# Toeplitz convolution of a gated attention kernel: the lower left 4x4 blocks by 12 block products with a shared term

## What is computed

```python
kv = jnp.einsum('bhil,bhjl->bijhl', k_, v_)
y = irfft(rfft(kv, n=2*L) * rfft(ssm_kernel, n=2*L), n=2*L)[..., :L]
out = y + kv * D[None, None, None, :, None]
out = jnp.einsum('bijhl,bhil->bjhl', out, q_)
x = x + jnp.tanh(g_xattn[0]) * out
```

## Time and profile before

| | |
|---|---|
| median of 3 runs | 1708.61 us (1708.61 to 1708.88) |
| the profiled execution | 1702.75 us, its span 1700.9 us |
| PE busy | 1553.1 us (91%) |
| DVE busy | 1232.6 us (72%) |
| POOL busy | 948.3 us (56%) |
| ACT busy | 538.7 us (32%) |
| mean granted clock of PE | 0.95 |

### The profile page before, as it was taken

One profiled execution on the slowest core, in us unless ns is written; L12 is line 12 of the kernel. 1 busy time (PEld: TensorE's weight loads), 2 busy tenths in 40 slices (PEclk: granted clock), 3 DMA queues, 4 the chain that ended last, 5 costly groups with the idle time before them and its releaser, 6 DMA issues. The chain is left out here.

```text
span 1700.9 us, 32688 instructions
## 1 busy us (share of the span) xinstructions
PE 1553.1 (91%) x11300; PEld 1494.9 (88%) x11301; DVE 1232.6 (72%) x1829; ACT 538.7 (32%) x848; POOL 948.3 (56%) x633
## 2 busy tenths in 40 slices
PE   5999999999999999999999999747999999996553
PEld 5999999999999999999999999647999999895332
DVE  4878888888888888888888888594444444444798
ACT  3333433333343334333333433203333333331000
POOL 6667757766775776577567757052222222232465
PEclk9999999999999999999999999857999999998586
DMA  5554554555455555545554554234788888885999
GB/s 182 166 178 158 172 170 163 177 177 175 154 170 167 173 165 189 165 152 174 173 176 157 181 167 146 79 133 137 251 291 311 288 305 292 299 276 196 411 396 360
DMA packets 101006, 350.84 MB, mean 206 GB/s; under 512 B 11953, under 2 KB 12465, under 8 KB 100977
## 3 DMA queue, kind: packets, MB, share of 16 engines
q1 hardware_dynamic: 71024, 241.39, 42.5%
q0 software_dynamic: 29952, 109.07, 18.0%
HBM read 236.58 MB, written 113.84 MB: 206 GB/s over the span
## 5 line engine op out<-in xcount | busy, mean ns | idle before, releaser
L584 PE MATMUL Y<-kvhi,t_hi 128*128 128x288 f32 x2304 | 689.4, 299 | 3.2 <-DMA t_lo<-klo 1.9
L584 PE MATMUL Y<-kvlo,t_hi 128*128 128x288 f32 x2304 | 679.9, 295 | 0.0
L584 PE MATMUL Y<-kvhi,t_lo 128*128 128x288 f32 x2304 | 679.8, 295 | 0.0
L584 PEld LDWEIGHTS Y<-kvhi,t_hi 128*128 128x128 f32 x2304 | 433.0, 188 | 4.9 <-DMA t_lo<-klo 2.3
L584 PEld LDWEIGHTS Y<-kvlo,t_hi 128*128 128x128 f32 x2304 | 433.7, 188 | 0.0
L584 PEld LDWEIGHTS Y<-kvhi,t_lo 128*128 128x128 f32 x2304 | 433.5, 188 | 0.0
L440 DVE TENSOR_REDUCE oT<-z 128x128 f32<-128x1280 f32 x256 | 379.5, 1482 | 6.7
L269 POOL TENSOR_TENSOR kvlo<-kv,kvhi 128x1152 fp32r<-128x1152 f32 x128 | 341.3, 2691 | 4.1 <-ACT kvhi L306 4.1
L423 DVE TENSOR_TENSOR z<-Y,qT 128x512 f32<-128x512 f32 x256 | 175.9, 687 | 174.1 <-PE Y L584 174.1
L258 POOL TENSOR_TENSOR kv<-cT 128x1024 f32<-128x1024 f32 x128 | 291.7, 2279 | 8.7 <-DMA cT<-in_c 8.7
L306 ACT CAST kvhi<-kv 128x1152 fp32r<-128x1152 f32 x128 | 148.5, 1161 | 303.3 <-POOL kv L261 303.3
(11 more groups left out here) (151 smaller groups left out, 2149.8 us busy)
## 6 DMA issues: line engine op xcount, KB each, us to landing
made_rows<-made POOLq DMA_DIRECT2D x72, 512.0 KB
t_hi<-khi SPq DMA_DIRECT2D x64, 512.0 KB, 3.9
t_lo<-klo SPq DMA_DIRECT2D x64, 512.0 KB, 5.1
cT<-in_c SPq DMA_DIRECT2D x32, 768.0 KB, 6.4
x_nat<-in_x SPq DMA_DIRECT2D x32, 512.0 KB, 4.1
x<-x_new SPq DMA_DIRECT2D x32, 512.0 KB, 4.9
normed<-n SPq DMA_DIRECT2D x32, 512.0 KB, 3.0
w_raw<-in_w SPq DMA_DIRECT2D x32, 384.0 KB, 4.1
```

The source lines that it names most:

```text
L584: mm = nc.tensor.matmul(Y[s2][:, a, 0:YC], t[h][:, w], m[h][:, s, :], start=(s == 0 and t is t_hi and m is kvhi), stop=(s == c and t is t_lo))
```

## The change

The lower left 4x4 blocks of the Toeplitz matrix (outputs 4 to 7, inputs 0 to 3) are seen as a 2x2 matrix of groups G of 2x2 blocks, G4 and G2 in the upper row, G6 and G4 in the lower (the number is the distance in blocks). Then

```diff
-ORDER = (1, 2, 0, 3)
+ORDER = (1, 2, 3, 0)
...
-        kv = [sb(f"kv{h}", [P, NC, YC]) for h in range(HT)]
+        kv = sb("kv", [P, NC, YC])
...
+                    eng.dma_start(u_hi[h][:].bitcast(F32), kernel_window(kshi_d, n, KS, SW)).then_inc(t_in[h], 16)
+                    eng.dma_start(u_lo[h][:].bitcast(F32), kernel_window(kslo_d, n, KS, SW)).then_inc(t_in[h], 16)
...
+                def difference(n):
+                    eng.wait_ge(square_done, 2 * n + 1)
+                    if not (isinstance(n, int) and n < 1):
+                        eng.wait_ge(diffhi_done, n)
+                    nc.gpsimd.tensor_tensor(diff[:], kv[:, 0:2, :], kv[:, 2:4, :], ALU.subtract).then_inc(diff_done, 1)
...
+                def low_difference(n, h):
+                    eng.wait_ge(diffhi_done, n + 1)
+                    nc.gpsimd.tensor_tensor(diff_lo[h][:], diff[:], diff_hi[h][:].bitcast(F32),
+                                            ALU.subtract).then_inc(difflo_done[h], 1)
...
-                    products(2 * i + h, h, 0, p, have)
-                    products(2 * i + h, h, 1, p, have)
+                    products(i, h, 0, p, have)
+                    products(i, h, 1, p, have)
+                    difference(2 * i + h)
+                    if isinstance(i, int) and i == 0 and h == 1:
+                        eng.wait_ge(k_out, 64)
                     low_kv(2 * i + h, h)
+                    low_difference(2 * i + h, h)
...
+                def squares(n, p, h):
+                    eng.wait_ge(kv_done, 2 * n + 1)
                     for half in range(2):
                         c0 = half * (NC // 2)
+                        nc.scalar.activation(kv[:, c0:c0 + NC // 2, 0:IB], cT[p][:, h, c0:c0 + NC // 2, 0:IB],
+                                             ACT.Square).then_inc(square_done, 1)
...
+                def head(n, p, h):
+                    squares(n, p, h)
+                    high_kv(n, h, 0)
+                    high_kv(n, h, 1)
+                    high_difference(n, h)
+
+                def take_common(n, h):
+                    eng.wait_ge(shared_ready, n + 1)
+                    if not (isinstance(n, int) and n < HT):
+                        eng.wait_ge(joined, 2 * n - 2)
+                    nc.scalar.copy(common[h][:], shared_y).then_inc(common_done, 1)
...
                 def body(i, p, first=False, last=False):
+                    take_common(2 * i, 0)
                     high_w(i)
-                    high_kv(2 * i + 1, 1)
+                    head(2 * i + 1, p, 1)
+                    if not first:
+                        root2(i - 1)
+                        normalize2(i - 1, 1 - p)
                     if not (isinstance(i, int) and i < 2):
                         take_small(i - 2)
-                    if not first:
-                        root2(i - 1)
+                    take_common(2 * i + 1, 1)
                     if not last:
-                        high_kv(2 * i + 2, 0)
-                    if not first:
-                        normalize2(i - 1, 1 - p)
-                    if not last:
+                        head(2 * i + 2, 1 - p, 0)
                         root(i + 1)
-                        normalize(i + 1, 1 - p)
                     if not first:
                         high_n2(i - 1)
                     if not last:
+                        normalize(i + 1, 1 - p)
                         take_q(i + 1, 1 - p)
...
+                    if n in (1, 2):
+                        eng.wait_ge(common_done, 2 * i + h + 1)
+                        nc.vector.tensor_tensor(y, y, common[h][:], (ALU.add, ALU.subtract)[n - 1]).then_inc(joined, 1)
+                        eng.wait_ge(joined, 4 * i + 2 * h + n)
...
                     multiply(i, p, 0, 1)
                     total(i, p, 0, 1)
                     if not first:
-                        residual(i - 1, 1 - p)
-                    multiply(i, p, 0, 2)
-                    if not first:
                         stats2(i - 1, 1 - p)
                         eng.wait_ge(n2st_done, 3 * i - 2)
+                    multiply(i, p, 0, 2)
+                    if not first:
+                        aggregate2()
                     total(i, p, 0, 2)
                     if not first:
-                        aggregate2()
+                        invert2(i - 1)
                     multiply(i, p, 0, 3)
-                    if not first:
-                        invert2(i - 1)
+                    if not (isinstance(i, int) and i < 2):
+                        take_lr(i - 2)
+                    total(i, p, 0, 3)
...
+                    total(i, p, 1, 0)
+                    if not first:
+                        low_n2(i - 1)
+                    multiply(i, p, 1, 1)
...
+                    shared(i, 0)
+                    conv(i, 0, 0)
+                    if not first:
+                        transpose_o(i - 1, 1 - p)
+                    conv(i, 0, 1)
+                    conv(i, 0, 2)
+                    if not (isinstance(i, int) and i < 2):
+                        project(i - 2)
+                    conv(i, 0, 3)
+                    shared(i, 1)
+                    conv(i, 1, 0)
+                    if not first:
+                        transpose_n2(i - 1, 1 - p)
+                    conv(i, 1, 1)
+                    conv(i, 1, 2)
                     if not last:
                         transpose_x(i + 1)
+                    conv(i, 1, 3)
```

More of the change, by code:

```diff
@@ L94, in attend @@
         qT = [sb(f"qT{p}", [P, HT, NC, WR]) for p in range(2)]
-        kv = [sb(f"kv{h}", [P, NC, YC]) for h in range(HT)]
+        kv = sb("kv", [P, NC, YC])
         kvhi = [sb(f"kvhi{h}", [P, NC, YC], F32R) for h in range(HT)]
         kvlo = [sb(f"kvlo{h}", [P, NC, YC], F32R) for h in range(HT)]
-        t_hi = [sb(f"t_hi{h}", [P, L], F32R) for h in range(HT)]
-        t_lo = [sb(f"t_lo{h}", [P, L], F32R) for h in range(HT)]
+        diff = sb("diff", [P, 2, YC])
+        diff_hi = [sb(f"diff_hi{h}", [P, 2, YC], F32R) for h in range(HT)]
+        diff_lo = [sb(f"diff_lo{h}", [P, 2, YC], F32R) for h in range(HT)]
+        t_hi = [sb(f"t_hi{h}", [P, TW], F32R) for h in range(HT)]
+        t_lo = [sb(f"t_lo{h}", [P, TW], F32R) for h in range(HT)]
+        u_hi = [sb(f"u_hi{h}", [P, SW], F32R) for h in range(HT)]
+        common = [sb(f"common{h}", [P, 2, YC]) for h in range(HT)]
+        u_lo = [sb(f"u_lo{h}", [P, SW], F32R) for h in range(HT)]
         oT = [sb(f"oT{p}", [P, NC, P]) for p in range(2)]
@@ L143, in attend @@
         kvlo_done = [sem(f"kvlo_done{h}") for h in range(HT)]
+        square_done = sem("square_done")
+        diff_done, diffhi_done = sem("diff_done"), sem("diffhi_done")
+        difflo_done = [sem(f"difflo_done{h}") for h in range(HT)]
+        shared_ready, common_done = sem("shared_ready"), sem("common_done")
+        joined = sem("joined")
         y_ready = sem("y_ready")
@@ L165, in attend, with kernel_window @@
         q_done = sem("q_done")
[L167 to L169 removed]
+        def kernel_window(d, n, row, width):
+            return bass.AP(tensor=d.tensor, offset=n * row, ap=[[1, P], [1, width]])
         stored = [lambda i: 8 * i, lambda i: 8 * i - 8]
@@ L367, in _ @@
                 eng.wait_ge(k_sum, 1)
-                nc.scalar.copy(krow_hi[:], krow[:]).then_inc(khi_done, 1)
+                nc.scalar.copy(krow_hi, krow).then_inc(khi_done, 1)
+                eng.wait_ge(ks_sum, 1)
+                nc.scalar.copy(ksum_hi, ksum).then_inc(kshi_done, 1)
                 eng.wait_ge(const_in, 48)
@@ L531, in body @@
                         eng.wait_ge(st_done, 3 * i + 4)
-                    total(i, p, 0, 3)
+                    multiply(i, p, 1, 0)
                     if not last:
                         aggregate(i + 1)
-                    if not (isinstance(i, int) and i < 2):
-                        take_lr(i - 2)
-                    multiply(i, p, 1, 0)
+                    total(i, p, 1, 0)
+                    if not first:
+                        low_n2(i - 1)
+                    multiply(i, p, 1, 1)
                     if not last:
                         invert(i + 1)
-                    total(i, p, 1, 0)
-                    multiply(i, p, 1, 1)
                     total(i, p, 1, 1)
                     multiply(i, p, 1, 2)
-                    if not first:
-                        low_n2(i - 1)
                     total(i, p, 1, 2)
@@ L567, in _, with block, shared, plain @@
             def _(eng):
+                def block(out, w_hi, w_lo, d, m_hi, m_lo, c, start=False, stop=False):
+                    w = slice(d * P, (d + 1) * P)
+                    nc.tensor.matmul(out, w_hi[:, w], m_hi[:, c, :], start=start, stop=False)
+                    nc.tensor.matmul(out, w_hi[:, w], m_lo[:, c, :], start=False, stop=False)
+                    return nc.tensor.matmul(out, w_lo[:, w], m_hi[:, c, :], start=False, stop=stop)
+                def shared(i, h):
```

(35 more changed lines are left out.)

106 lines of the change are left out of this document (63 added, 43 removed).

## The result

| | before | changed |
|---|---|---|
| median | 1708.61 us | 1718.3 us (1717.02 to 1718.95) |
| ratio | | 1.0059, interval 1.0042 to 1.0077 |
| span of the profiled execution | 1700.9 us | 1717.0 us |
| PE / DVE / POOL / ACT busy | 1553 / 1233 / 948 / 539 us | 1498 / 1332 / 1068 / 656 us |
| mean granted clock of PE | 0.950 | 0.927 |

The changed kernel is slower by 0.6%; 1686 was forecast. The profiled execution of before was 6 us faster than its median, and its stages after the first took 598.5 us, where the traces of all the other kernels here, with the same code there, have 600.8 to 603.9. So of the 16.1 us between the two spans only 9.7 are in the difference of the medians.

The account below looks back on a forecast made before the run. The relay over ACT and POOL, with xn, was taken as the new bound: 32.3 us a tile against 33.27. Thirty tiles at 0.94 gain 28.2; with the ends the net is -22.5, so 1686 us, range 1660 to 1740.

Parts of the forecast that it names:

- The full 100 us of PE's queue: Matmuls on PE: queue falls 3.2 us to 29.95 a tile, 100 us if PE still set the pace.
- PE's own loop through the relay: PE's work together with the relay, from tile to tile: 32.1 us, next late after the loop of 32.3.
- the relay: From shared(i,0)'s end over ACT's take_common, w_hi and POOL's w_lo, products, difference, low_kv, low_difference to shared(i,1): 16.0 us.
- the relay with xn in it: Relay, then high_n2, DVE's low_n2 to invert, ACT's xn, transpose_x, next shared: 32.3 us a tile, the bound; chance 0.44.
- the join: DVE's add of 576 elements with one operand and result in PSUM, four a tile: 0.75 us each.
- rival 6: Table loads on ACT if Square lies outside Sqrt's table: +2.0 us a tile, +39 us, 1748; chance 0.06.
- The 0.24 for slower: Chance that the changed kernel is measured slower, from the join, clock and table load cases.
- the three rivals: The slower cases: join's PSUM read and write taking turns (0.10), PE's clock (0.07), ACT's table loads (0.06).
- rival 5: PE's clock falls to 1.2 GHz once a tile after 2.1 us idle: 34.0 a tile, +29 us, 1738; chance 0.07.
- the loops over xn: DVE's loop, queue 30.6 plus 0.8 idle and handoffs: 31.4 to 31.9; relay with xn: 32.3 a tile.
- rival 2: DVE or PE through the relay binds at 31.6 a tile, handoffs being shorter: 45 us less, 1664; chance 0.17.
- the ends: Stage's start and end: +4.6 start, +0.5 first tile, +0.6 tile 1, -1.2 last tile, +1.2 DVE's arrears.

Follow-up runs that it names:

- c1_invert: The changed kernel with one call moved: DVE's invert(i+1) ahead of low_n2; 1689.36 us, 0.9893 of the kernel before.
- b1_fill_order: a1_fill with DVE's invert(i+1) moved ahead of low_n2 and ACT's take_small ahead of root2; 1689.71 us, 0.9892 of the kernel before.
- a1_fill: The changed kernel with 12 extra matmuls a tile, result overwritten, in PE's idle time ahead of shared(i,1); 1699.26 us, 0.9956 of the kernel before.
- a2_relay: The changed kernel with ACT's high_w after head(2i+1) and POOL's low_w after head(i,1); 1690.83 us, 0.9906 of the kernel before.
- c4_halffill: a1_fill with 6 extra matmuls instead of 12, ahead of shared(i,1); 1699.4 us.
- a3_relay_nojoin: a2_relay with DVE's four joins a tile replaced by an operation on one element; 1682.09 us, 0.986 of the kernel before.

## Why the prediction was wrong

**Right.** The full 100 us of PE's queue did not come, because loops over other engines took over, and PE's own loop through the relay, forecast at 32.1, measures 32.31 (c1_invert) and 32.33 (b1_fill_order). That this equals the 32.3 forecast for another loop, the relay with xn in it, is luck: that loop takes 32.7 (below). Most terms held: the join 0.76 to 0.77 for 0.75, POOL's part of the relay 14.3 (498.85 to 513.19) for 14.2, its wait for w_hi 5.6 to 8.4 instead of 10.23, the first shared matmul at 25.48 for 25.8, 24 matmuls less a tile. PE idles 1.7 to 2.1 before shared(i,1), forecast 2.1. There are no loads of a table within the tiles, which ends rival 6. The Trainium skill (ScalarE: Activation LUTs, Table sets) has cheap functions in every set; the trace is in line with it, and shows of Square that it alternates with Sqrt here without a load. The 0.24 for slower holds the 0.01 of the change not doing what it says; the three rivals add up to 0.23.

**Wrong, first: rival 5, the clock, had a chance of 0.07.** I took the 2.21 us row, at full clock, as the nearest, read the 0.80 behind it as the end of a series, and so the sum priced the relay's idle time at nothing. That was a misreading: the row shows only the first matmul after the idle time, and the clock falls later. Windows of the kernel before (window, length, busy of PE, clock, DMA share, GB/s) around the row at 1627.61:

```profile
1627.00:1628.00 1.00, 0.40 (x2) 1.00 1.04 426
1628.00:1629.00 1.00, 1.00 (x6) 0.93 1.05 373
1629.00:1630.00 1.00, 0.48 (x2) 0.50 0.96 385
...
1631.00:1632.00 1.00, 0.31 (x1) 0.50 1.00 401
```

Some 1.3 us after PE had gone on the clock went to 0.50, and the 0.80 at 1631.69 was taken at that clock. In the changed kernel the falls come 1.0 to 1.4 us after PE has gone on, in 14 of 29 tiles. The size was off as well, in the other direction: a fall costs 1.24 us, not 1.9, since the low stretch is 3 us instead of 3.9 and a little of it runs under slack. 14 x 1.24 = 17 us in steady tiles; a1_fill shows 19 in all. The Trainium skill (TensorE: Matmul & The Clock Gate, HAM oscillation) had warned of idle time repeated in a loop, with a kernel whose waits took 3 to 5 us and whose every pass started cold. The trace agrees in part: falls came with 1.77 to 2.09 us, in 14 of 29 passes, and each pass started at full clock.

**Wrong, second: the loops over xn, a term of the sum.** DVE's was put at 31.4 to 31.9 and is 32.66. From one multiply of (0,0) to the next it runs 18.02 on DVE (500.29 to 518.31), 2.83, 1.14 and 2.06 to invert at 524.34, then 1.81 to transpose_x at 526.15 and 6.88 over the last convolution, shared and the next first convolution: 32.74. The prediction had summed DVE's queue and one wait and added half a microsecond for handoffs; laid out in order, two waits behind bn_stats (0.22 and 0.19), 0.9 instead of 0.8 at take_lr, and 8.7 us over ACT and PE were more than that. a2_relay is the proof: without the relay the tile stays at 32.65.

The relay with xn in it, which the sum took at 32.33, was short as well. In the same tile it takes 16.16 from the end of shared(i,0) at 497.13 to shared(i,1) (forecast 16.03), 12.86 to transpose_x (12.70) and 3.72 to the next end of shared (3.60): 32.74. The two loops meet in low_n2, and they are tied: DVE starts it 0.03 us after the end of ACT's n_hi in every tile, 0.03 to 0.05 later than its own queue would let it (1.43 to 1.45 after the start of the reduce, elsewhere 1.40). Timeline of ACT; low_n2 is the row at 521.14 above:

```profile
519.82 0.20 ACT L380 ACTIVATE low<-mv 128x1 f32<-128x1 f32 x1
...
520.11 0.99 ACT L428 CAST n_hi<-XP 128x1024 fp32r<-128x1024 f32 x1
```

At full clock ACT's part of this waits now for DVE, now for its own casts of the relay, with some 0.15 us at most between them. So shortening the relay alone gained nothing in a steady tile at full clock (a2_relay); shortening DVE's loop alone would gain some 0.1 us, an estimate from these rows that no run tests; c1_invert shortens both. The term costs 0.33 x 29 = 10 us. "DVE binds" stood as rival 2, but with the sign of a gain, at 31.6.

**Wrong, third: the ends.** Net +5.7 was said; the third take_q comes 8.4 us later than before (4.8 expected at that point) and the stage's last stretch is 4.0 us longer (0 expected). Low clock again: in tiles 0 and 1 stretches of 5.3 and 5.5 us at 0.50 follow PE's waits of 4.02 and 3.57 us. The runs fit this: with both stretches the third take_q is at 94.25 (c4_halffill), with one of some 3 us at 90.60 (a1_fill), with none at 85.76 (a2_relay). At the end one more fall comes in the last tile, PE waits longer for DVE, and it is slower in its transposes than before (2.97 and 1.58 us):

```profile
1098.91 1.97 PE L709 MATMUL OP<-const_ident,oT 128*128 128x128 f32 x8 [5.35 <-DVE oT L515]
```

The wait is 2.4 us longer than before; the prediction had put DVE's arrears at 1.2. No run takes the 4.0 us apart.

Together 10 + 17 + 3.6 + 4.0 = 35 us above a forecast of -22.5: +12 at the end of this stage, where the trace has +13.1. The other 3 us of the two spans are in the later stages, whose code is the same in both.

**The order of the calls decided the sign.** The same instructions with four calls moved (high_w, low_w, take_small, invert) take 1647.87, 3.5% less than the kernel before.

## What to carry to other kernels

Where one engine's queue is shortened, lay out every loop over the others in the order of their queues, with each handoff, before the gain is counted; the sum of a queue plus a lump for handoffs was short by 0.8 us in 32 here, and moving one call (invert, take_small, high_w with its low_w) was worth 15 to 29 us, but two of them together only some 10 where the relay stood close behind (b1_fill_order). Idle time of TensorE is not free where it stands off the critical loop: recurring in one piece of some 2 us it cost the clock here, and filling it, even by half, ended that. Read the clock of the stretch behind an idle time, not the length of the first matmul. And price the stand-in of an ablation before it is run: only taking the instruction out altogether told what the joins cost.

## What the runs showed of the hardware

- TensorE's clock fell to 0.50 some 1.0 to 1.4 us after the end of an idle time of 1.77 to 2.09 us in 14 of 29 tiles, and did not in the 15 others with 1.74 to 2.10 (changed kernel), nor with 1.68 to 1.72 in any of 30 (c1_invert), nor with 1.78 at another place in the tile (a2_relay). What chooses among tiles with the same idle time is open; no run tells the length from the place.
- A fall took 3 us at half speed and cost 1.24 us of a tile of 32.66.
- VectorE's add with one operand and the result in PSUM, 128x576, took 0.76 us, on the line of the operations that write SBUF.
- An operation of VectorE on one element, with the next instruction waiting for it, took 0.66 us in the median in a3_relay_nojoin (0.33 to 1.02 in 122 of 128 rows), where the reciprocal of this size takes 0.15 (L531 above). Why, was not tried.
